# Adjacency signs as bytes, turned two tiles at a time, and the features of round one wholly on GpSimd

## The reference

```python
feat_1 = x @ a[:Fdim]
feat_2 = x @ a[Fdim:]
e = jax.nn.leaky_relu(feat_1 + feat_2.T, ALPHA)
U = jax.nn.softmax(jnp.where(adj > 0, e, NEG_INF), axis=1)
prop_u = U @ x
rowsum = jnp.sum(U * (0.5 * U), axis=1)
coe = jax.nn.sigmoid(temp)
feat = coe[2] * (prop_u - x * rowsum[:, None]) + (1 - coe[2]) * (x + prop_u - x * rowsum[:, None])
feat = jnp.where(jnp.abs(feat) > THRESH, jnp.abs(feat) - THRESH, 0.0) * jnp.sign(feat)
pu = U @ feat
...
```

## Time and profile before

| | us |
|---|---|
| median of 3 runs | 868.73 (866.7 to 872.04) |
| profiled execution, own time | 869.0 |
| its span, first to last instruction | 867.3 |
| TensorE busy | 800.7 (92%) |
| VectorE busy | 749.8 (86%) |
| ScalarE busy | 676.8 (78%) |
| GpSimd busy | 581.1 (67%) |

### The profile page before, as it was taken

The page is one execution under the profiler, slowest core; times in us unless marked ns, Lnnn a source line. Parts: engine busy times, 40 slices in busy tenths (PEclk is TensorE's granted clock), DMA queues, the critical chain, the costliest instruction groups (busy, mean ns, idle before and its releaser), DMA issues. The chain is left out here.

```text
span 867.3 us, 22265 instructions
## 1 busy us (share of the span) xinstructions
PE 800.7 (92%) x6654; PEld 763.9 (88%) x6654; DVE 749.8 (86%) x1966; ACT 676.8 (78%) x1402; POOL 581.1 (67%) x1220
## 2 busy tenths in 40 slices
PE   3977999998999899997899999999999999999956
PEld 1667999998999899997789999999999999999945
DVE  6558899996999799988699999999999999999852
ACT  6667888876877787895588888888888898898751
POOL 4462366654666566675588887787787787788850
PEclk9689999998999999999899999999999999999975
DMA  6446979786878687622211112111111111110000
GB/s 197 135 158 188 309 228 297 241 278 201 272 243 276 231 254 261 202 98 66 62 62 65 46 57 67 39 63 60 42 63 60 42 63 60 39 43 14 8 3 10
DMA packets 97547, 110.74 MB, mean 128 GB/s; under 512 B 6464, under 2 KB 89280, under 8 KB 97472
## 3 DMA queue, kind: packets, MB, share of 16 engines
q1 hardware_dynamic: 97472, 109.74, 39.8%
HBM read 90.85 MB, written 18.87 MB: 127 GB/s over the span
## 5 line engine op out<-in xcount | busy, mean ns | idle before, releaser
L1121 ACT ACTIVATE maskA<-code 128x1024 fp32r<-128x1024 int8 x256 | 268.4, 1051 | 49.5 <-DVE code L688 26.6
L1387 PE MATMUL accA<-Y,maskA 128*128 128x260 f32 (+1 forms) x1792 | 274.7, 297 | 18.7 <-ACT maskA L1121 13.4
L1397 PE MATMUL accC<-Y,maskC 128*128 128x260 f32 (+1 forms) x1792 | 256.4, 286 | 1.8 <-DVE maskC L696 1.8
L1387 PEld LDWEIGHTS accA<-Y,maskA 128*128 128x128 f32 x1792 | 236.7, 194 | 21.7 <-ACT maskA L1121 14.2
L1397 PEld LDWEIGHTS accC<-Y,maskC 128*128 128x128 f32 x1792 | 232.7, 192 | 2.7 <-DVE maskC L696 2.7
L688 DVE SCALAR_TENSOR_TENSOR code<-f_rows,neg_f,ps 128x512 int8<-128x512 f32 x256 | 178.6, 741 | 40.7 <-PE ps L1327 39.3
L696 DVE TENSOR_SCALAR maskC<-code 128x1024 fp32r<-128x1024 int8 x256 | 212.2, 830 | 0.0
L1061 ACT ACTIVATE edges<-adj_in 128x1024 bf16<-128x1024 f32 x128 | 133.1, 1045 | 22.9 <-DMA adj_in<-in_adj_dram 17.0
L593 POOL TENSOR_TENSOR room_r<-room,room_r 128x256 fp32r<-128x256 f32 x128 | 94.3, 765 | 2.5
L1327 PE MATMUL ps<-ident,edges 128*128 128x128 bf16 x1024 | 82.2, 225 | 12.7 <-ACT edges L1061 9.2
L956 DVE SCALAR_TENSOR_TENSOR room<-room 128x128 f32<-128x128 f32 x288 | 92.2, 342 | 0.0
(11 more groups left out here) (230 smaller groups left out, 1625.4 us busy)
## 6 DMA issues: line engine op xcount, KB each, us to landing
adj_in<-in_adj_dram SPq DMA_DIRECT2D x128, 512.0 KB, 4.6
edge_codes<-code SPq DMA_DIRECT2D x8, 2048.0 KB, 9.6
code<-edge_codes SPq DMA_DIRECT2D x32, 512.0 KB, 3.3
xn<-in_x_dram SPq DMA_DIRECT2D x4, 512.0 KB, 5.6
room<-in_x_dram SPq DMA_DIRECT2D x32, 64.0 KB, 1.8
room<-in_L_gnn_h_dram SPq DMA_DIRECT2D x32, 64.0 KB, 1.9
out_dram<-room SPq DMA_DIRECT2D x32, 64.0 KB, 1.6
room<-in_L_ffn_W_in_dram SPq DMA_DIRECT2D x1, 192.0 KB, 2.7
```

The lines of the kernel that those rows point to most:

```text
L1121: s.activation(maskA[:, b % MASKS], src, ACT.Relu, bias=-2.0).then_inc(S["maskA_ready"], 1)
L1387: t_.matmul(accA[k][:, 0:2 * cols], maskA[:, b % MASKS, l * P:(l + 1) * P], y2_of(jt, 0) if cols == F else Y[:, jt, 0, :, 0:cols], start=j ...
L1397: m = t_.matmul(accC[k][:, 0:2 * cols], maskC[:, b % MASKS, l * P:(l + 1) * P], y2_of(jt, 1) if cols == F else Y[:, jt, 1, :, 0:cols], sta ...
```

## The change

The adjacency's signs are written as bytes by a rectified multiply: 2 for no edge, and 127 (saturated) for an edge. The bytes of column w of two neighbouring column tiles lie side by side and are read as one bf16 word, so one matmul by the identity (now 1 on the diagonal) turns both tiles; a bank holds the words of a block, and the code operation reads the third or fourth byte of each. `edges` has 8 slots of half the width. The code is now the comparison (0 or 1) minus the byte, and the masks take -126 and -127. `turn` does four matmuls in place of eight and fills one bank; it waits for the bank of four blocks ago.

`feat1` is gone. GpSimd computes the row in `features`, with `scaled_done` raised before the row's operations, `feat_done` raised by GpSimd, and `feature_sum(T - 1)` in place of T - 2. The column of squares, `q_c`, is computed by ScalarE in `read_acc` from the accumulator and a table of squared weights, made once.

```diff
-        edges, Y2_2a = shared("edges", [P, 4, IT, 2 * P], BF16, [("Y2_2a", [P, JB, 2, F], F32R)])
+        edges, Y2_2a = shared("edges", [P, EDGE_SLOTS, IT, P], BF16, [("Y2_2a", [P, JB, 2, F], F32R)])
...
             def features(T, k):
...
-                wait(pool, "feat_done", T - 1)
-                if not isinstance(T, int) or T >= 2:
-                    feature_sum(T - 2)
+                g.sem_inc(S["scaled_done"], 1)
+                if not isinstance(T, int) or T >= 1:
+                    feature_sum(T - 1)
+                mine = xn[:, bass.ds(row, 1), :].rearrange("p a b -> p (a b)")
                 link(g.tensor_tensor(k_one[:, k], coef[:, 5:6], n["rho"], ALU.subtract))
                 link(g.tensor_tensor(featw[:, 0], col_mean[:], n["zn"].broadcast_to([P, F]), ALU.mult))
-                link(g.tensor_tensor(featw[:, 1], featw[:, 0], num[:, 0:F], ALU.add))
-                link(g.tensor_tensor(scaled[:, k], featw[:, 1], n["r"].broadcast_to([P, F]), ALU.mult))
+                link(g.tensor_tensor(featw[:, 1], mine, k_one[:, k].broadcast_to([P, F]), ALU.mult))
+                link(g.tensor_tensor(featw[:, 0], featw[:, 0], num[:, 0:F], ALU.add))
+                link(g.tensor_tensor(featw[:, 0], featw[:, 0], n["r"].broadcast_to([P, F]), ALU.mult))
+                link(g.tensor_tensor(featw[:, 0], featw[:, 0], featw[:, 1], ALU.add))
+                link(g.tensor_scalar(featw[:, 1], featw[:, 0], -THRESH, THRESH, ALU.max, ALU.min))
+                link(g.tensor_tensor(mine, featw[:, 0], featw[:, 1], ALU.subtract))
+                g.sem_inc(S["feat_done"], 1)
                 link(g.tensor_copy(row_out[:, bass.ds(row, 1), :].rearrange("p a b -> p (a b)"), small[:, 2:6]))
                 end_chain()
-                g.sem_inc(S["scaled_done"], 1)
...
+            def turned(jt):
+                words = ps[jt // JH % TRB][:, :].bitcast(I8)
+                return words.rearrange("p (i r y) -> p i r y", i=IT, y=4)[:, :, :, 2 + jt % JH]
...
-                    scalar=neg_f2[:, jt:jt + 1], in1=ps[jt % TRB][:, :].rearrange("p (i r) -> p i r", i=IT),
-                    op0=ALU.is_gt, op1=ALU.add).then_inc(S["coded"], 1)
+                    scalar=neg_f2[:, jt:jt + 1], in1=turned(jt),
+                    op0=ALU.is_le, op1=ALU.subtract).then_inc(S["coded"], 1)
...
-                v.tensor_scalar(q_c[:, k], both[:, :, F + 1], w, w, ALU.mult, ALU.mult)
...
-            def feat1(T, k):
...
-            feat1(NT - 3, 1)
+            dve.wait_ge(S["feat_done"], NT - 2)
...
-                    act.wait_ge(S["tr_done"], n * 2 - 6)
-                s.activation(edges[:, h % 4], adj_in[:, h % 4], ACT.Sign).then_inc(S["signed"], 1)
+                    wait(act, "tr_done", (n - EDGE_SLOTS + 1) * JH)
+                pair = edges[:, h % EDGE_SLOTS].bitcast(I8).rearrange("p i (w e) -> p i e w", e=JH)
+                s.activation(pair, adj_in[:, h % 4].rearrange("p i (e w) -> p i e w", e=JH), ACT.Relu, bias=FREE, scale=HUGE).then_inc(S["signed"], 1)
...
-                s.activation(maskA[:, b % MASKS], src, ACT.Relu, bias=-2.0).then_inc(S["maskA_ready"], 1)
+                s.activation(maskA[:, b % MASKS], src, ACT.Relu, bias=1.0 - LINK, scale=-1.0).then_inc(S["maskA_ready"], 1)
...
+                if not round_two:
+                    squares = accC[k][:, 0:2 * cols].rearrange("p (a b) -> p a b", a=2)[:, :, F + 1]
+                    s.mul(q_c[:, k], squares, roww_sq[:, bass.ds(row, 1)])
...
-                for j in range(JH):
-                    jt = b * JH + j
-                    if not (first and jt < TRB):
-                        pe.wait_ge(S["coded"], G * NT + (jt - TRB + 1))
-                    for it in range(IT):
-                        m = t_.matmul(ps[jt % TRB][:, it * P:(it + 1) * P], edges[:, b % 4, it, j * P:(j + 1) * P], ident2[:], start=True, stop=True)
-                    m.then_inc(S["tr_done"], 1)
+                if not (first and b < TRB):
+                    pe.wait_ge(S["coded"], G * NT + (b - TRB + 1) * JH)
+                for it in range(IT):
+                    m = t_.matmul(ps[b % TRB][:, it * P:(it + 1) * P], edges[:, b % EDGE_SLOTS, it], ident2[:], start=True, stop=True)
+                m.then_inc(S["tr_done"], JH)
```

More of the change, by code:

```diff
@@ L33 @@
 EPS = 1e-05
+HUGE = 1e30
+FREE = 2.0
+LINK = 127.0
 SLOPE = 0.2
@@ L48, in gnn_ffn_kernel @@
     TRB = 4
+    EDGE_SLOTS = 8
     assert F == P and NG % 2 == 0
@@ L110, in gnn_ffn_kernel @@
         roww = sb("roww", [P, NT, 2])
+        roww_sq = sb("roww_sq", [P, NT])
         hcol = sb("hcol", [P, 2, NT])
@@ L419, in _ @@
             link(g.memset(ident[:], 0.0))
-            g.affine_select(out=ident2[:], in_=ident2[:], compare_op=ALU.not_equal, fill=2.0, base=0,
+            g.affine_select(out=ident2[:], in_=ident2[:], compare_op=ALU.not_equal, fill=1.0, base=0,
                             pattern=[[-1, P]], channel_multiplier=1)
@@ L516, in _ @@
                     features(u * 2 + k, k)
-            pool.wait_ge(S["feat_done"], NT - 3)
-            feature_sum(NT - 4)
-            pool.wait_ge(S["feat_done"], NT - 2)
             feature_sum(NT - 3)
@@ L689, in codes @@
                     out=code[par][:, :, jt * P:(jt + 1) * P], in0=f1_rows[:, rows].rearrange("p (i r) -> p i r", i=IT),
-                    scalar=neg_f2[:, jt:jt + 1], in1=ps[jt % TRB][:, :].rearrange("p (i r) -> p i r", i=IT),
-                    op0=ALU.is_gt, op1=ALU.add).then_inc(S["coded"], 1)
+                    scalar=neg_f2[:, jt:jt + 1], in1=turned(jt),
+                    op0=ALU.is_le, op1=ALU.subtract).then_inc(S["coded"], 1)
             def mask_c(n, src, b):
                 wait(dve, "mm_done", n - (MASKS - 1))
-                v.tensor_scalar(maskC[:, b % MASKS], src, 2.0, None, ALU.is_equal).then_inc(S["maskC_ready"], 1)
+                v.tensor_scalar(maskC[:, b % MASKS], src, 1.0 - LINK, None, ALU.is_equal).then_inc(S["maskC_ready"], 1)
             def mask1(G, par, b):
@@ L748, in supertile @@
                         sum1(G * IT + (it - 1), (it - 1) % 2)
-                    if ch == 2 and not (first and it < 2):
-                        feat1(G * IT + (it - 2), it % 2)
             chain = [0]
@@ L816, in _ @@
                     sum1(G * IT + (it - 1), (it - 1) % 2)
-                if ch == 2 and it < IT - 1:
-                    feat1(G * IT + (it - 2), it % 2)
                 for t in Y2_AT[b]:
@@ L1183, in _ @@
                     s.activation(roww[:, :, 0], hcol[:, 0], ACT.Exp, bias=-SHIFT, scale=-1.0)
+                    s.activation(roww_sq[:], hcol[:, 1], ACT.Exp, scale=-2.0)
                     s.activation(roww[:, :, 1], hcol[:, 1], ACT.Exp, scale=-1.0).then_inc(S["roww_done"], 1)
```

## The result

The changed kernel took 884.02 us (median; 882.82 to 885.36) against 870.29 us (866.70 to 872.04) for the kernel before on the same chip: a ratio of 1.0164, with a 95% interval of 1.0123 to 1.0205. It is slower by 1.6%. The forecast was 890, range 862 to 910. The profiled execution took 885.36 us, its span 883.6, which is 16.3 us longer than the span of before; the working had given 21.2.

A forecast was written before the change was run, and what follows sets the result against it. GpSimd's chain was taken to bound round one at 11.27 us a tile. Start -2.4, tiles +29.3 and end -5.7 gave +21.2 us on the profiled 869.0, 890.2, forecast as 890, range 862 to 910.

The forecast's parts named there:

- The bound: Round one: GpSimd's chain sets the pace, 11.27 us a tile against TensorE's 8.87 plus its edges; chance 0.62.
- The slack of two tiles: Round one: double-buffered sums, readings and `k_one` give some 11 us of slack, used up after five or so tiles.
- The period: GpSimd's time per tile in round one: 11.27 us against 10.26 before, +29.3 us over tiles 0 to 28.
- The hits on the port: Round one: GpSimd operations lengthened by VectorE's masks on the shared port, some 1.4 us of the old chain's 8.12.
- the prediction's figure from below, 8.67: GpSimd's old chain per tile without idle time, low estimate: 8.12 us plus the step to the next tile.
- the middle of 9.0: GpSimd's old chain per tile without idle time, taken as 9.0 us between 8.67 and 9.32.
- The start: Ahead of `features(0)`: it starts 2.4 us earlier, 1.5 from the prologue and 0.9 from four blocks.
- The end: From the start of `features(29)` to TensorE's restart: 15.9 us in place of 21.6, so -5.7.
- The free port: Rival, round one: VectorE's masks hit GpSimd less, period 9.6 us without any hit, about 842 us; chance 0.12.
- The half-way case of 10.2 to 10.8: Rival, round one: GpSimd's period of 10.2 to 10.8 us gives 858 to 876 us; chance 0.15.
- The clock: Rival, round one: TensorE's lower clock, at 0.75 a tile of 11.8 us, +14 us; 904 to 929; chance 0.08.
- Slow bytes: Rival, round one: bytes read from PSUM take twice as long, 14 us a tile, +118, 987 us; chance 0.03.

The follow-up runs named there:

- the first experiment: The changed kernel with the three operations of `feat1` back on VectorE, all else as in the change: 845.57 us, ratio 0.9735.

## Why the prediction was right

The mechanism was the one forecast, and its sum of 21.2 us stands against 16.3 measured. Term by term:

*The bound.* Right: GpSimd back to back, ScalarE's reading waiting for it 61.9 us in total (40 to 60 expected, 2.7 us each where some 2 were put), its own wait for the sums 22.7 (some 25 expected). One sign missed: TensorE was to be under 85% busy, and it is 84 and 89% in the two stretches shown and 86% from 160 to 360 us, with a granted clock of 0.96, 0.91 and 0.94; at a lower clock the same work fills more of the time. The slack of two tiles didn't hide it: ScalarE first waits 2 us for GpSimd at 142.16, in the fifth tile, where the prediction had "after five or so tiles".

*The period.* 11.27 us expected, 11.18 measured; 29 x (11.18 - 10.26) = +26.7 where the sum had +29.3. The nearness is in part luck, as two errors stand against each other. The four operations were taken as 2.27 us and are 2.48: the clamp, taken as 0.40 between 0.23 and 0.46, took 0.65, above both bounds, while the small extras before a register's row came out as put. The hits on the port were taken as 11.27 less 9.57 (7.3 + 2.27), 1.7 us, and are 1.4, which is what the prediction itself had counted from its rows. The unhindered period, put at 9.6, is 9.70, so the old chain is 9.70 - 2.48 = 7.22 without hits (7.3 was put) and some 8.6 with them: the prediction's figure from below, 8.67, was right for round one, and the middle of 9.0 was 0.4 too long.

*The start.* -2.4 expected, -4.2 measured. The prologue gave more than the 1.5 taken off it (between 0 and 5); in the other kernels with the bytes the start is 3.8 to 7.7 us earlier, so this term is uncertain by some 4 us from one kernel to the next.

*The end.* -5.7 expected, -5.8 measured (21.59 to 15.81): the last sum and its scalars do run beside the chain. That it fits so well is luck. GpSimd ended that tile's subtraction at 425.00, 9.56 us after the tile began, where the sum had 10.4, and from there to the restart it was 6.25 us, where it had 5.5:

```profile
424.54 0.46 POOL L511 TENSOR_TENSOR xn<-featw 128x128 f32 x1
```

Together -4.2 + 26.7 - 5.8 = +16.7, which is TensorE's restart (+16.6). Round two is unchanged.

*The rivals.* The free port fell: with the port nearly free, in the run with narrow masks, the time was 847, near the 842 worked out for it, and 1.4 us of hits a tile keep the change away from that. The half-way case of 10.2 to 10.8 didn't come either. The run without the threshold, at 10.03, lies just below it, and took 853; the prediction's sum gives 853 for that period too. The clock: after the stall at 321.49 TensorE's eight products at L1392 took 1.93 us instead of 1.11, and the granted clock of a stretch fell to 0.91; but the pace of GpSimd is nearly the same with TensorE's longer or shorter turning (11.29 and 11.18), so this lay inside TensorE's waiting. Slow bytes fell with the 744 and 1055 ns.

The expectations of the runs were weaker than the prediction in one place: for the first experiment I put the gain of the bytes and rings at the steady tile's 0.3 us and 4 us at the start, and the kernel was 10 us better. The steady tile was sized rightly (9.88 to 9.56). What was missing was that the pace of 10.26 had the two stalls at the loop's edges in it, and that they would go.

## What to carry to other kernels

An engine whose chain takes 8.1 of 9.7 us does not have 1.6 us to give: 0.4 to 0.7 of that is its step to the next tile, so it is 1.1. Put 2.5 us of work there and the steady tile grows by the difference (9.7 to 11.1 here), however much it frees elsewhere. Before moving work, add to the receiving engine's chain its steps between linked operations and the hits on a shared port, and compare the sum with the new period of the bound. Don't go by the engine's share of busy time, which was 73% over the whole program and 76% in round one for the engine that set the pace. Look at every period and not only at their mean, since two long ones can hold half of what there is to win. Take apart a change that bundles a gain and a loss: the bytes and rings alone are 2.5% faster, the move of the features alone 2.7% slower.

## What the runs showed of the hardware that I had not expected

The clamp on GpSimd, one input and two operations with immediate numbers over 128 elements a partition, takes 0.65 us where an addition of two such rows takes 0.46 (L510 and L509 above). VectorE does the same clamp in 0.23 us, less than its subtraction of two rows, as its timeline in the first experiment shows:

```profile
383.97 0.23 DVE L733 TENSOR_SCALAR fwork<-fwork 128x128 f32<-128x128 f32 x1
384.24 0.29 DVE L734 TENSOR_TENSOR xn<-fwork 128x128 f32<-128x128 f32 x1
```

The Trainium skill, "GPSIMD Engine Reference", section 4.1 Engine selection, has GpSimd some 2 times slower than VectorE for two inputs and roughly at line rate for one. Here it is the other way round for this pair: 0.46 against 0.29, a factor of 1.6, for two inputs, and 0.65 against 0.23, a factor of 2.8, for one input with two operations. One input with a single operation wasn't measured at this size.

Two bytes in one 16-bit word go through TensorE's turning at the price of one (0.21 us a block in place of 0.43), and neither the write of every second byte by ScalarE (1055 ns for 1024 elements) nor the read of every fourth from PSUM by VectorE (744 ns for 512) costs more than 1% over what whole words did (1045 and 741 ns).
